# An attention and mixture-of-experts layer on one core: last iterations rearranged, turned rows in PSUM, x in four loads, last pairs added ahead

## What is computed

```python
def reference(x, ctx_1024, g_xattn, g_ffn, ...):
    x = x + tanh(g_xattn[0]) * attention(layernorm(x), ctx_1024, ctx_1024, Wq, bq, Wk, bk, Wv, bv, Wo, bo)
    xf = layernorm(x).reshape(-1, 256)
    scores = softmax(xf @ w_router)
    expert_weights, expert_indices = top_k(scores, 2)
    y_e = (silu(xf @ w1[e]) * (xf @ w3[e])) @ w2[e]            # hidden size 512
    moe_out = sum over the token's two experts of weight * y_e
    shared = silu(xf @ ws1) * (xf @ ws3) @ ws2
    return x + tanh(g_ffn[0]) * (shared / 3 + moe_out * 2 / 3)
```

## Time and profile before

| | |
|---|---|
| median of 3 runs | 824.37 us (824.17 to 826.52) |
| the profiled execution, its own time | 821.54 us |
| its span in the trace | 819.8 us |
| PE busy | 771.5 us, 94% |
| DVE, POOL, ACT busy | 543.3, 432.0, 413.4 us |
| mean granted clock of TensorE | 0.994 |
| chain that ended last | PE 51%, POOL 14%, DMA 13%, issue 9%, DVE 7% |

### The profile page before, as it was taken

The page is one execution under the profiler, slowest core; times in us unless marked ns, Lnnn a source line. Parts: engine busy times, 40 slices in busy tenths (PEclk is TensorE's granted clock), DMA queues, the critical chain, the costliest instruction groups (busy, mean ns, idle before and its releaser), DMA issues.

```text
span 819.8 us, 19446 instructions
## 1 busy us (share of the span) xinstructions
PE 771.5 (94%) x6977; PEld 688.4 (84%) x6978; DVE 543.3 (66%) x1118; ACT 413.4 (50%) x690; POOL 432.0 (53%) x486
## 2 busy tenths in 40 slices
PE   4889999999999999988998999999999999999997
PEld 4766777777777766568998999999999999999996
DVE  5677789998888898946564444444444444456787
ACT  5767776777777776742334324343333343333331
POOL 5633446666666655466571566656757584236000
PEclk9999999999999999999999999999999999999999
DMA  6855556766666653253487343324333422218522
GB/s 205 275 179 164 187 182 229 227 225 216 211 213 208 206 175 124 96 183 130 146 231 265 75 128 85 113 68 119 99 106 82 121 53 75 54 57 327 219 81 74
DMA packets 129102, 127.34 MB, mean 155 GB/s; under 512 B 55184, under 2 KB 110992, under 8 KB 129040
## 3 DMA queue, kind: packets, MB, share of 16 engines
q1 hardware_dynamic: 114896, 80.34, 32.8%
q0 software_dynamic: 14144, 46.19, 16.1%
HBM read 75.32 MB, written 50.91 MB: 154 GB/s over the span
## 4 chain that ended last, share of the span: by engine, by line
PE 51%; POOL 14%; DMA 13%; issue 9%; DVE 7%; ACT 4%; SPq 2%; POOLq 1%; ACTq 0%; DVEq 0%
PE bank L561 6%; POOL w_l L1610 6%; PE bank_ss L613 5%; PE bank L563 5%; PE bank L562 5%; DMA y_d<-y_s,y_rows 5%; PE bank L642 5%; DMA y_rows<-xs_d 4%; PE bank_sm L626 4%; PE bank_sm L561 3%; PE bank_sm L562 2%; PE bank_sm L563 2%; PE bank_ss L561 2%; PE bank L649 2%; PE bank_ss L563 2%
## 5 line engine op out<-in xcount | busy, mean ns | idle before, releaser
L1247 DVE TENSOR_REDUCE row_max<-bank_sm 128x4 f32<-128x1024 f32 x124 | 151.5, 1222 | 38.2 <-PE bank_sm L626 36.8
L952 ACT ACTIVATE probs_T<-bank_ss 128x1024 f32<-128x1024 f32 x123 | 126.4, 1027 | 18.8 <-PE bank_ss L613 18.5
L1226 DVE TENSOR_TENSOR gT_l<-gg,gT_h 128x1024 fp32r<-128x1024 f32 x49 | 66.7, 1360 | 103.1 <-ACT gT_h L1083 103.1
L561 PE MATMUL bank_sm<-xg_h,w_h 128*128 128x256 f32 x400 | 115.1, 288 | 4.5 <-DVE xg_l L1226 4.4
L561 PE MATMUL bank<-w_h,gT_h 128*128 128x256 f32 x392 | 111.4, 284 | 3.2 <-DVE gT_l L1226 3.2
L562 PE MATMUL bank_sm<-xg_h,w_l 128*128 128x256 f32 x400 | 114.4, 286 | 0.0
L563 PE MATMUL bank_sm<-xg_l,w_h 128*128 128x256 f32 x400 | 114.3, 286 | 0.0
L561 PE MATMUL bank_ss<-xg_h,w_h 128*128 128x256 f32 x400 | 113.2, 283 | 0.0
L562 PE MATMUL bank_ss<-xg_h,w_l 128*128 128x256 f32 x400 | 112.9, 282 | 0.0
L563 PE MATMUL bank_ss<-xg_l,w_h 128*128 128x256 f32 x400 | 112.9, 282 | 0.0
L562 PE MATMUL bank<-w_h,gT_l 128*128 128x256 f32 x392 | 110.9, 283 | 0.0
(11 more groups left out here) (203 smaller groups left out, 1951.7 us busy)
## 6 DMA issues: line engine op xcount, KB each, us to landing
qk_d<-qk_s SPq DMA_DIRECT2D x64, 256.0 KB, 3.0
w_raw<-wall POOLq DMA_DIRECT2D x27, 512.0 KB, 3.9
k<-qk_d SPq DMA_DIRECT2D x48, 256.0 KB, 4.1
q<-qk_d SPq DMA_DIRECT2D x48, 256.0 KB, 4.6
xq<-xs_d SPq DMA_DIRECT2D x140, 64.0 KB, 2.2
y_pairs<-y_d POOLq DMA_DIRECT2D x16, 512.0 KB, 8.8
x<-x SPq DMA_DIRECT2D x16, 256.0 KB, 4.7
c_s<-ctxT SPq DMA_DIRECT2D x16, 256.0 KB, 3.0
```

Of the source, the lines that this page charges most:

```text
L561: pe.matmul(out, ah, bh, start=first and k == 0, stop=False)
L952: act.activation(pT[:, 2 * (pv % 4):2 * (pv % 4) + 2, :].rearrange("p h t -> p (h t)"), exp_bank(V.b, pv)[:, :], ACT.Exp, scale=D ** -0.5) ...
L1226: return v.tensor_tensor(dst, ps, high.bitcast(F32), ALU.subtract)
L1247: v.tensor_reduce(mx[B.slot][:, :, :].rearrange("p t (r q) -> p r t q", r=2)[:, :, :, p], max_bank(B.b, p)[:, :].rearrange("p (r t k) -> p ...
```

## The change

It does the following.

- Behind the last iteration, `logits` of batches 13 and 14 write T2 and not T1, PE's wait for `lgc_ok` ahead of `project_out` goes, and one for batch 14 is put ahead of `down(0)`. PE does `down(0)` and `up1(2)` ahead of `turn_norm(x15)`. The count matmul stands behind `up1(3)`.
- ACT copies `head_out(x15, 3)` ahead of `silu(0)`. POOL does `root` for batches 14 and 15 ahead of a cut. DVE does `x_low_shared` of tiles 2 and 3, `gated(2)` and `g_low(2)` earlier in the row.
- `turn_rows` writes bank 4; ACT and DVE read it there. For routed tile 0 it stands ahead of `gated(5)`.
- x_all is loaded in four parts, one behind each of the first four experts.
- Both pairs of batch 15 and of batch 14 are added to x_all in tiles 11 to 14, between `gated` and `g_low`; batch 14's last sum is one operation into the output tile.
- In iteration -1, stats and variance of batch 3 stand ahead of the first `row_max`. The filler matmuls have 512 columns and half the count: 14, 4 and 4 in place of 28, 8 and 8.
- `logits` and `best_two` get the bank's columns as an argument `at`, with no other change to them.

```diff
--- before.py
+++ after.py
@@ -49,6 +49,7 @@
 WP = 3
+X2_PARTS = 4
 PVW = 32
@@ -239,7 +240,6 @@
             xq = sb(m, "xq", [P, TR // QD, FQ])
-            xrT = sb(m, "xrT", [P, EC, TR])
             y_s = sb(m, "y_s", [P, TS, E])
@@ -268,6 +268,7 @@
         rk_tail = bank[4][:, 0:TC * NX]
+        lg_tail = T2[:, TC * NX:2 * TC * NX]
         psX, psY, psH1, psH3 = bank[4], bank[5], bank[2:4], bank[0:2]
...
@@ -827,8 +828,7 @@
             values(x15, 2)
-            logits(x13)
-            pe.wait_ge(lgc_ok, x13.n(1, 1))
+            logits(x13, lg_tail)
             project_out(x14)
@@ -842,25 +842,26 @@
             up1(1, SHARED)
-            logits(x14)
-            pe.wait_ge(lgc_ok, x14.n(1, 1))
+            logits(x14, lg_tail)
             project_out(x15)
...
             pe.wait_ge(pos_ok, NB - 3)
+            pe.wait_ge(lgc_ok, x14.n(1, 1))
             down(0, SHARED)
+            up1(2, SHARED)
             turn_norm(x15)
-            up1(2, SHARED)
-            logits(x15)
             up3(2, SHARED)
+            logits(x15, lg_p)
+            down(1, SHARED)
             rank(x15, rk_tail)
-            down(1, SHARED)
-
-            pe.wait_ge(acc_ok, NB)
-            pe.matmul(T0[:, 0:NX], counters[:, 1, :], acc[:, 0, :], start=True, stop=True).then_inc(cnt_ps, 1)
+
             for g in range(3, EARLY):
                 up1(g, SHARED)
+                if g == 3:
+                    pe.wait_ge(acc_ok, NB)
+                    pe.matmul(T0[:, 0:NX], counters[:, 1, :], acc[:, 0, :], start=True, stop=True).then_inc(cnt_ps, 1)
                 up3(g, SHARED)
@@ -1068,7 +1069,7 @@
                 act.wait_ge(h3_ps, g)
-                act.activation(xg_h[:, :, :], xrT[:, :, :], ACT.Copy).then_inc(xh_ok, 1)
+                act.activation(xg_h[:, :, :], psX[:, :].rearrange("p (c t) -> p c t", c=EC), ACT.Copy).then_inc(xh_ok, 1)
@@ -1099,8 +1100,8 @@
             probs(x15, PAIRS - 1)
+            head_out(x15, 3)
             silu(0)
-            head_out(x15, 3)
             x_high_shared(1, 1)
...
@@ -1332,10 +1333,22 @@
+                def stats_ahead():
+                    v.wait_ge(x_in[Eb.b % 2], 16 * (Eb.b // 2) + 16)
+                    stats(x_s[Eb.x_slot], bst)
+
+                def variance_ahead():
+                    moved(v, xn_ok, Eb.n())
+                    mean_and_variance(bst, bmv)
+                    add_eps(bmv, var1_ok)
+
                 def before(p):
+                    if p == 0 and Eb and Eb.b == R:
+                        stats_ahead()
+                        variance_ahead()
                     if p == 2 and S3:
-                        best_two(S3)
+                        best_two(S3, lg_p)
                     if p == 4 and S2:
@@ -1347,18 +1360,15 @@
-                    if p == 0 and Eb:
-                        v.wait_ge(x_in[Eb.b % 2], 16 * (Eb.b // 2) + 16)
-                        stats(x_s[Eb.x_slot], bst)
+                    if p == 0 and Eb and Eb.b != R:
+                        stats_ahead()
                     if p == 0 and S4:
...
                         list_slots(S4)
-                    if p == 1 and Eb:
-                        moved(v, xn_ok, Eb.n())
-                        mean_and_variance(bst, bmv)
-                        add_eps(bmv, var1_ok)
+                    if p == 1 and Eb and Eb.b != R:
+                        variance_ahead()
                     if p == 2 and S3:
@@ -1409,13 +1419,12 @@
                 v.wait_ge(xl_ok, g)
-                v.transpose(xrT[:, :, :].rearrange("p c (t q) -> p c t q", q=QD),
+                v.transpose(psX[:, :].rearrange("p (c t q) -> p c t q", c=EC, q=QD),
                             xq[:, :, :].rearrange("p t (c j) -> p c t j", c=EC)).then_inc(xt_ok, 1)
             def x_low_routed(g):
-                turn_rows(g)
                 v.wait_ge(xh_ok, g + 1)
-                low(xg_l[:, :, :], xrT[:, :, :], xg_h[:, :, :]).then_inc(xl_ok, 1)
+                low(xg_l[:, :, :], psX[:, :].rearrange("p (c t) -> p c t", c=EC), xg_h[:, :, :]).then_inc(xl_ok, 1)
...
@@ -1445,30 +1454,30 @@
             gated(0)
-            best_two(x14)
+            best_two(x14, lg_tail)
             masks(x14)
...
             positions(x14, rk_tail)
+            x_low_shared(2, 2)
             list_slots(x14)
-            x_low_shared(2, 2)
             norm(x15)
             gated(1)
             g_low(1)
-            best_two(x15)
+            best_two(x15, lg_p)
             masks(x15)
+            x_low_shared(3, 3)
+            gated(2)
             positions(x15, rk_tail)
             list_slots(x15)
-            x_low_shared(3, 3)
-            gated(2)
+            g_low(2)
...
             v.tensor_copy(tab[0:1, T_Z:T_Z + NX], tabf[0:1, T_Z:T_Z + NX]).then_inc(ends_ok, 1)
-            g_low(2)
             gated(3)
@@ -1504,6 +1513,8 @@
             g_low(4)
+            v.wait_ge(pos_ok, NB)
+            turn_rows(EARLY)
             gated(5)
@@ -1511,6 +1522,7 @@
             end = v.value_load(tab[0:1, T_E + NX - 1:T_E + NX], min_val=EARLY + 2 * NX, max_val=EARLY + NT)
+            turn_rows(EARLY + 1)
             x_low_routed(EARLY + 1)
@@ -1518,6 +1530,7 @@
             with v.Fori(EARLY + 1, last) as g:
+                turn_rows(g + 1)
                 x_low_routed(g + 1)
@@ -1546,16 +1559,28 @@
+            def add_pair(b, k):
+
+                v.wait_ge(yg_in[b], 16)
+                settle()
+                for t in range(TS):
+                    at = x2a[:, b, t * E:(t + 1) * E]
+                    r = v.scalar_tensor_tensor(at, yg[:, b, t, k, :], wts[:, TS * b + t, k:k + 1], at, ALU.mult, ALU.add)
+                mark(r)
+
+            PAIR_AT = {NB - 5: (NB - 1, 0), NB - 4: (NB - 1, 1), NB - 3: (NB - 2, 0), NB - 2: (NB - 2, 1)}
             x_low_shared(EARLY, end)
             gated(last)
             g_low(last)
-            v.wait_ge(x2_in, 16)
+            v.wait_ge(x2_in, 16 * X2_PARTS)
             for j in range(EARLY // 2):
...
                     gated(end + (j - EARLY))
+                    if j in PAIR_AT:
+                        add_pair(*PAIR_AT[j])
                     g_low(end + (j - EARLY))
@@ -1570,18 +1595,18 @@
                     settle()
-                else:
+                elif j < NB - 1:
                     add_late(j - 1)
                 for b in mixed_at(j):
-                    mix(b)
-
+                    if b < NB - 2:
+                        mix(b)
+
+            b = NB - 2
+            settle()
+            v.wait_ge(w2_ps, end + (b + 1 - EARLY))
+            v.wait_ge(o_st[b % 2], (b // 2) * 16)
+            v.scalar_tensor_tensor(o_o[b % 2][:, :, :].rearrange("p t d -> p (t d)"), psY[:, :], gsc[:, 0:1], x2a[:, b, :], ALU.mult, ALU.add).then_inc(mix_ok, 1)
             b = NB - 1
-            v.wait_ge(yg_in[b], 16)
-            for k in range(2):
-                for t in range(TS):
-                    at = x2a[:, b, t * E:(t + 1) * E]
-                    r = v.scalar_tensor_tensor(at, yg[:, b, t, k, :], wts[:, TS * b + t, k:k + 1], at, ALU.mult, ALU.add)
-                link(r)
             v.wait_ge(o_st[b % 2], (b // 2) * 16)
@@ -1706,13 +1731,13 @@
             po.wait_ge(mx_ok, NB * PAIRS)
+            root(bmv2, rstd2, var2_ok, x14, rstd2_ok)
             cut(1, 0, which=(0,))
-            root(bmv2, rstd2, var2_ok, x14, rstd2_ok)
             scatter(x13, 0)
             scatter(x13, 1)
             po.wait_ge(oh_ok, x14.n(1, 1))
+            root(bmv2, rstd2, var2_ok, x15, rstd2_ok)
             cut(1, 0, which=(1,))
-            root(bmv2, rstd2, var2_ok, x15, rstd2_ok)
             scatter(x14, 0)
@@ -1725,9 +1750,6 @@
             cut(2, 1)
-            po.wait_ge(x2_st, NB * 16)
-            po.dma_start(x2a[:, :, :], x2_d.rearrange("b p d -> p b d")).then_inc(x2_in, 16)
-
             def scatter_y(g):
@@ -1753,6 +1775,10 @@
                     scatter_y(g)
+                if e < X2_PARTS:
+                    n = NB // X2_PARTS
+                    po.wait_ge(x2_st, NB * 16)
+                    po.dma_start(x2a[:, e * n:(e + 1) * n, :], x2_d[e * n:(e + 1) * n].rearrange("b p d -> p b d")).then_inc(x2_in, 16)
             total = po.value_load(tab[0:1, T_N:T_N + 1], min_val=2 * NX, max_val=NT)
```

22 lines of the change are left out of this document (11 added, 11 removed).

## The result

The changed kernel took 816.1 us in the median of four runs (812.4 to 819.1), against 824.9 for the kernel before on the same chip: a ratio of 0.9885, 95% interval 0.9848 to 0.9921. In a later comparison it took 812.3 us in the median of six (808.0 to 815.4): 0.9854, interval 0.9819 to 0.9889. So it is 9 to 12 us faster where 15.0 had been forecast; both medians are above 809.4, the first one is also just above the range's end (815.5). The profiled execution has a span of 812.4 us: 7.4 less than the earlier trace rows.

A forecast was written before the change was run, and what follows sets the result against it. PE was busy 771.5 of 819.8 us, the rest waits, with some work at a low clock. Terms 0.4 + 7.1 + 1.8 + 4.05 - 1.2 + 2.85 = 15.0 took the median 824.37 to 809.4 us, range 805.5 to 815.5.

The forecast's parts named there:

- Ramp, +0.4: In the ramp, batch 3's stats and variance go ahead of row_max, where DVE is idle: gain 0.4 us, between 0 and 1.0.
- Attention's end, 7.1: Where attention ends and shared tiles begin, PE's waits and a low clock go: gain 7.1 us, between 4.5 and 8.6.
- It came at 365.43 where it could have come at 360.85: At attention's end, POOL's root of batch 14 goes ahead of a cut, so norm comes about 4 us earlier.
- 2.37 and 2 x 0.75: At attention's end, PE's wait ahead of turn_norm(15), 2.37 us, and its two for best_two, 0.75 us each, go.
- The 1.7 of clock: At attention's end, the low clock behind PE's wait of 2.37 us goes with it: 1.7 us.
- Routed tile 0, 1.8: Before routed tile 0, the earlier turn_rows leaves a chain of about 2.1 us that fits under down(4): gain 1.8 us.
- Routed tile 3, 4.05: Before routed tile 3, the wait of 2.35 us behind the 4 MB x load and 1.7 us of clock go: 4.05 us.
- Rival B: The next wait, at routed tile 0, takes attention's end's gain; 2 of 7.1 stay, clock falls once: 816.2 us; 10 in 100.
- x in four loads, loss of 1.2: At expert changes, four issues on POOL's queue cost 3.0 us, and xg_l slowing cuts less returns 1.75: loss of 1.2.
- expert waits of 4 to 5 us in sum: Sign for the changed profile: PE's waits at changes of expert come to 4 to 5 us in sum.
- Rival A: Split x loads hold up scatter_y or its row numbers at four expert changes, 6.1 us each: 832.6 us; 4 in 100.
- The end, 2.85: Behind PE's last matmuls, eight DVE operations go, so the last STT ends at 814.65 instead of 817.49: gain 2.85 us.

The follow-up runs named there:

- fillers: The changed kernel with the filler matmuls back to 28, 8 and 8 of 256 columns: 818.29 us, 0.9935 of the kernel before.
- rows_first: The changed kernel with an own buffer for the first routed tile's rows, and rows of tiles 0 and 1 loaded ahead of SP's zero fills: 807.57 us, 0.9803.
- cut_between: rows_first with POOL's two cuts of the first expert's weights moved from behind the roots to between the two scatters of a batch: 804.94 us, 0.9767.
- joint_undone: rows_first with the end of attention as in the kernel before (old bank, old orders on PE and DVE, silu(0) first, cuts ahead of roots): 809.23 us, 0.9815.
- rf_one: rows_first with x in one load of 4 MB, as in the kernel before: 823.89 us, 0.9985 of the kernel before.

## Why the prediction was right, and where it was wrong

*Direction and size.* The direction is right: 0.9885 and 0.9854, for most of the reasons named. The size was 7.4 and 9.5 us in the two profiles, for 15.0. Part of that is luck: fillers shows 6 us that come from the wide fillers, which the sum puts at nothing, and they make up for part of what the wait at tile 1 and attention's end took away.

*Ramp, +0.4.* The move itself gave more. From the end of the wait for q (near 30 us) to the fillers behind row_max took 10.3 us in both profiles of the kernel before, and 9.5 in the second profile of the changed kernel and in rows_first. PE's wait for row_max stayed (0.63 and 0.64 for 0.67), since PE comes to it earlier too. Whether 0.8 us last to the end is not decided. The logits of the last iteration start at 339.0 and 340.6 in the two profiles of the kernel before and at 338.4 to 343.8 in the changed one's family, which had up to four low clocks before 350 each. But "the filler matmuls keep their columns, so I give them nothing" is wrong: narrow fillers in place of the wide ones cost 6 us on the changed kernel and 10 on rows_first.

*Attention's end, 7.1.* From the logits of the last iteration to shared tile 5 the changed kernel gained 5.5 and 4.4 us on the first profile of the kernel before, and each of its profiles has a low clock of 1.7 us in this stretch, as the kernel before has: the low clock behind the old wait is gone, and another stands there. PE came to routed tile 0 5.9 and 6.1 us earlier, not 9. Two steps failed. "It came at 365.43 where it could have come at 360.85": root 14 came at 363.30 and, in the second profile, at 361.35, since POOL was in a scatter that had waited for a landing; and norm, which I took at its free duration, took 2.45 us beside the cut:

```profile
364.08 2.45 DVE L1314 TENSOR_SCALAR xn<-x_s,bn_mv,rstd 128x256 f32<-128x256 f32 x2 [0.50 <-POOL rstd L1653]
...
366.44 1.75 DVE L1227 TENSOR_TENSOR xg_l<-xsT,xg_h 128x512 fp32r<-128x512 f32 x1
```

So PE waited 1.09 + 1.01 us (1.84 + 1.01 in the second profile) where I had one wait for xg_l, and 0.54 for gg. The rule of the Trainium skill (SBUF — State Buffer, Who interferes with whom) that I weighed against the rows was right: norm beside the copy and the first subtraction of a cut took 2.44 to 2.47 us in all ten profiles where the two meet, and 0.74 in cut_between, joint_undone and both of the kernel before. It held for small ones too: slot_i's CAST 1.10 instead of 0.17 us in rows_first. I should have counted with it. That 2.37 and 2 x 0.75 go, and that no wait takes their place, was right. cut_between, with no wait over 0.45 us and no low clock there, gained 8.9 us in this stretch, so the 7.1 were there to be had. The 1.7 of clock in that sum is real in both profiles of the kernel before, but joint_undone has the same wait without it.

*Routed tile 0, 1.8.* Right: no wait. *Routed tile 3, 4.05.* Right on its own terms: with the rows of tile 1 out of the way both together give 5.3 of 5.85, and rf_one shows what the 4 MB load does to row loads.

*What I left out* is what cost most: the turn that I moved ahead of gated also frees xq, and so moves SP's next load into the zero fills. The sum holds no term for it. I had worked out the slack of tile 0's rows, and not what a turned tile releases. It cost 6.1 us and 1.8 us of clock in one profile, 3.6 and 1.7 in the other. Rival B said that the next wait would take the gain, put it at tile 0 and came to 816.2; it came one tile later and by another way. "Wrong if a wait of over 2 us stands at tile 0 or at an expert change, or a slow clock between 350 and 700": no such wait stood there, but the slow clock did, at 425 to 435, and at 365 to 370 in the second profile. By its own sign the forecast failed, at a place that it had not looked at.

*x in four loads, loss of 1.2.* Wrong in sign in both profiles, small in size: the changed kernel gained 2.2 and 1.4 us in this stretch, and rf_one against rows_first shows that the loads themselves are neutral there (261.1 and 261.6). What makes up the rest is within what two profiles of the kernel before differ by (1.4). The sign "expert waits of 4 to 5 us in sum" was wrong too: 1.5. Rival A did not come: each load landed in 6.2 to 6.9 us, and the longest expert wait is 0.57 us in the first profile and 1.40 in the second, below. *The end, 2.85:* 3.0 to 3.1 in all profiles.
